# Window attention with a pooled branch: one copy of x, one trip of statistics, key sums on GpSimd, seeds in PSUM

## What is computed

```python
def _gn(v, G=32, eps=1e-05):
    g = v.reshape(B_, G, C_ // G, H_, W_)
    m = jnp.mean(g, axis=(2, 3, 4), keepdims=True)
    s = jnp.var(g, axis=(2, 3, 4), keepdims=True)
    return ((g - m) / jnp.sqrt(s + eps)).reshape(v.shape)

xr = x.reshape(B, H, W, C)                      # a reshape, no transpose
g = window_attn(xr, Wqkv, bqkv, scale) @ Wproj + bproj
l = xr.reshape(B, C, H // 2, 2, W // 2, 2).mean(axis=(3, 5))
l = window_attn(l.reshape(B, h, w, C), Wqkv, bqkv, scale).reshape(B, C, h, w)
lx = 0.5 * (px[:, :, :-1, :] + px[:, :, 1:, :])    # px: l, padded by reflection
ly = 0.5 * (py[..., :-1] + py[..., 1:])
l = jax.image.resize(lx + ly, (B, C, H, W), method='bilinear')
return (g + l.reshape(B, H, W, C)).transpose(0, 3, 1, 2)

x = x + _L0_conv_ref(_gn(x), Wqkv, bqkv, Wproj, bproj)
```

## Time and profile before

| What | Value |
|---|---|
| median of 3 runs | 93.77 us (93.16 to 94.08) |
| span of the profiled execution, first to last instruction | 92.3 us |
| the profiled execution's own time | not given apart; median minus span is 1.5 us |
| busy: PE, VectorE, ScalarE, GpSimd | 79.7, 61.6, 36.6, 26.9 us |
| HBM read, written | 5.11 MB, 2.10 MB |

### The profile page before, as it was taken

One profiled execution on the slowest core, in us unless ns is written; L12 is line 12 of the kernel. 1 busy time (PEld: TensorE's weight loads), 2 busy tenths in 40 slices (PEclk: granted clock), 3 DMA queues, 4 the chain that ended last, 5 costly groups with the idle time before them and its releaser, 6 DMA issues.

```text
span 92.3 us, 1700 instructions
## 1 busy us (share of the span) xinstructions
PE 79.7 (86%) x620; PEld 62.0 (67%) x620; DVE 61.6 (67%) x101; ACT 36.6 (40%) x80; POOL 26.9 (29%) x50
## 2 busy tenths in 40 slices
...
PEclk9999999999999999999999999999999999999999
...
GB/s 6 248 254 251 228 322 404 415 87 0 7 0 0 0 4 0 11 0 0 0 0 0 7 0 0 0 0 0 7 0 227 0 0 4 7 0 227 0 227 227
DMA packets 3464, 7.32 MB, mean 79 GB/s; under 512 B 896, under 2 KB 1152, under 8 KB 3456
## 3 DMA queue, kind: packets, MB, share of 16 engines
...
HBM read 5.11 MB, written 2.10 MB: 78 GB/s over the span
## 4 chain that ended last, share of the span: by engine, by line
PE 74%; DMA 9%; ACT 3%; POOL 3%; DVE 2%; issue 2%; ACTq 2%; DVEq 1%
PE ot_ps L755 14%; PE q_ps L681 9%; PE v_ps L691 9%; DMA xr<-in_x 9%; PE k_ps L672 6%; PE job_ps L771 6%; PE s_ps L713 6%; PE ot_ps L739 5%; PE job_ps L778 5%; PE job_ps L644 4%; PE k_ps L771 2%; ACT xn L431 2%; PE job_ps L656 2%; PE k_ps L778 2%; ACT xt L447 1%
## 5 line engine op out<-in xcount | busy, mean ns | idle before, releaser
L542 DVE TENSOR_TENSOR qk<-q_sb,k_ps 128x1536 f32<-128x1536 f32 x10 | 17.3, 1737 | 2.7 <-ACT q_sb L460 2.7
L410 POOL TENSOR_TENSOR out_sb<-out_sb,xc 128x512 f32<-128x512 f32 x4 | 6.0, 1512 | 40.9 <-ACT out_sb L482 40.9
L590 DVE TENSOR_TENSOR pv<-prob_w,v_ps 128x1536 f32<-128x1536 f32 x9 | 15.7, 1739 | 0.7 <-PE ot_ps L755 0.7
L755 PEld LDWEIGHTS ot_ps<-ident,pv 128*128 128x128 f32 x120 | 13.7, 141 | 3.3 <-issue 3.0
L755 PE MATMUL ot_ps<-ident,pv 128*128 128x128 f32 x120 | 14.9, 273 | 0.0
L477 ACT ACTIVATE ot<-ot_ps,bias_qkv 128x512 f32<-128x512 f32 x10 | 6.9, 687 | 12.8 <-PE ot_ps L755 12.8
L497 DVE BATCH_NORM_STATS2 bn<-xr 128x6 f32<-128x512 f32 x8 | 5.5, 682 | 6.6 <-DMA xr<-in_x 6.6
L681 PE MATMUL q_ps<-xt,w_sb 128*128 128x512 f32 x16 | 9.3, 665 | 0.5 <-ACT xt L447 0.5
L691 PEld LDWEIGHTS v_ps<-w_sb,xt 128*128 128x128 f32 x64 | 7.9, 192 | 1.0 <-issue 1.0
L691 PE MATMUL v_ps<-w_sb,xt 128*128 128x128 f32 x64 | 8.5, 275 | 0.0
L278 POOL TENSOR_TENSOR xn<-xn 128x384 f32<-128x384 f32 x6 | 6.0, 1000 | 8.0 <-ACT xn L431 8.0
...
## 6 DMA issues: line engine op xcount, KB each, us to landing
...
```

The lines of the kernel that those rows point to most:

```text
L542: nc.vector.tensor_tensor(qk[:, m % 2, :, :, n % 2, :], q, k, ALU.mult).then_inc(qk_done, 1)
L590: nc.vector.tensor_tensor(to, p, v, ALU.mult).then_inc(pv_done, 1)
L755: ins = nc.tensor.matmul(view[:, q // 2, q % 2], pv[:, n % 2, q, k, :], eye, is_transpose=True, start=(sums == KEYS and q == 0), stop=last ...
```

## The change

- x is loaded once, by channels (`xc`), one load per image on SP's queue, and serves statistics, pooling, normalising and the last addition. `wp_sb` moves from ScalarE's queue to SP's. `resize_sb` has 8 blocks for 10.
- Statistics: two `bn_stats` and one `bn_aggr` per image, the mean of squares made on VectorE (`ag`), one small matmul per image (`st`), four small VectorE operations (`ps`), the power on GpSimd (`pw`), offset and scale on VectorE (`of`).
- Transposes (`T`) read the channel copy; token 0 is subtracted after the transpose (`df`): on VectorE out of PSUM for tiles 0 to 3, on GpSimd in SBUF for the other six, where ScalarE's `xe` copies all 512 columns (128 for tiles 0 to 3).
- Value 0 of an image tile is projected with the operands exchanged, so that its features lie on the partitions; ScalarE adds the bias (`ve`) and writes it twice for each half of a bank (`sd`), and `O` accumulates on it. `v0` is gone.
- GpSimd adds the three products of the keys in SBUF (`H`, two operations of 128 x 512 for tiles 0, 2, 3, 4, 6, 7 and 8, three with value 0 for the pooled tiles 1 and 5, none for tile 9), so that `O` has 4 transposes for 12, but for tile 9. Pooled tiles get another 2 (`Om`, to the copy `mid`).
- ScalarE writes x and the output bias into the result's bank ahead (`sx`); `L` (4 blocks for 5) and `W` accumulate on it, and a copy (`R`) goes out, on ScalarE but for (3, 0) on VectorE. `add` is gone; image 3 is stored whole.
- The sum of exponents is made by two additions instead of a reduction. Four banks (`a_ps`) are shared by T, Q, K, V, O by a table, three (`b_ps`) by seeds and results; `pv` has four buffers. The pooled tiles stand second and sixth, and `ORDER` is new.

```diff
-TILES = [(0, 0), (0, 1), (1, 0), (None, 0), (1, 1), (2, 0), (None, 1), (2, 1), (3, 0), (3, 1)]
...
+TILES = [(0, 0), (None, 0), (0, 1), (1, 0), (1, 1), (None, 1), (2, 0), (2, 1), (3, 0), (3, 1)]
...
+PV = [1, 3, 0, 2, 3, 1, 0, 2, 0, 3]
...
+ORDER = {
+    "PE": [
+        ("st", 0), ("st", 1), ("T", 0), ("T", 2), ("st", 2), ("Q", 0), ("T", 1), ("K", 0), ("Q", 2), ("Q", 1),
+        ("T", 3), ("st", 3), ("K", 1), ("zero",), ("T", 4), ("K", 2), ("Q", 3), ("S", 0), ("K", 3), ("T", 6),
+        ("T", 9), ("V", 0), ("T", 7), ("S", 1), ("T", 5), ("V", 1), ("Q", 6), ("Q", 4), ("Q", 7), ("T", 8), ("K", 7),
+        ("Q", 9), ("K", 6), ("Q", 5), ("K", 5), ("K", 4), ("S", 3), ("V", 3), ("O", 1), ("O", 0), ("V", 2), ("Om", 1),
+        ("S", 2), ("K", 9), ("V", 4), ("Q", 8), ("L", 1, 0), ("O", 3), ("V", 5), ("W", 1, 0), ("V", 7), ("O", 2),
+        ("V", 6), ("L", 0, 0), ("L", 0, 1), ("K", 8), ("W", 0, 1), ("W", 0, 0), ("O", 4), ("S", 4), ("L", 1, 1),
+        ("V", 9), ("Om", 5), ("O", 5), ("W", 1, 1), ("O", 7), ("L", 2, 1), ("V", 8), ("W", 2, 1), ("O", 6), ("O", 9),
+        ("L", 2, 0), ("W", 2, 0), ("L", 3, 1), ("L", 3, 0), ("O", 8), ("W", 3, 1), ("W", 3, 0),
+    ],
+    "DVE": [
+        ("bn", 0), ("ag", 0), ("bn", 1), ("ps", 0), ("ag", 1), ("bn", 2), ("of", 0), ("nm", 0, 0), ("ps", 1),
+        ("ag", 2), ("df", 0), ("of", 1), ("df", 2), ("ps", 2), ("bn", 3), ("df", 1), ("ag", 3), ("M", 0), ("of", 2),
+        ("ps", 3), ("df", 3), ("M", 1), ("of", 3), ("M", 2), ("X", 0), ("M", 3), ("D", 0), ("U", 0), ("X", 1),
+        ("P", 0), ("P", 1), ("D", 1), ("M", 7), ("M", 6), ("M", 5), ("M", 4), ("U", 1), ("X", 3), ("P", 3), ("P", 2),
+        ("X", 2), ("M", 9), ("D", 2), ("D", 3), ("U", 2), ("P", 4), ("P", 5), ("M", 8), ("U", 3), ("P", 7), ("X", 4),
+        ("P", 6), ("D", 4), ("U", 4), ("P", 9), ("P", 8), ("R", 3, 0),
+    ],
+    "ACT": [
+        ("nm", 0, 1), ("xe", 0), ("pn", 0), ("xe", 2), ("pn", 1), ("Qo", 0), ("xe", 1), ("nm", 1), ("Qo", 2),
+        ("Qo", 1), ("xe", 3), ("xe", 4), ("nm", 2), ("Qo", 3), ("nm", 3), ("pn", 3), ("xe", 6), ("E", 0), ("xe", 9),
+        ("pn", 2), ("xe", 7), ("ve", 0), ("sd", 0), ("xe", 5), ("ve", 1), ("E", 1), ("Qo", 6), ("Qo", 4), ("Qo", 7),
+        ("xe", 8), ("Qo", 9), ("sx", 1, 0), ("Qo", 5), ("oo", 1), ("ve", 3), ("sd", 3), ("oo", 0), ("om", 1),
+        ("ve", 2), ("ve", 4), ("sx", 0, 0), ("E", 2), ("Qo", 8), ("oo", 3), ("E", 3), ("sd", 2), ("oo", 2), ("ve", 5),
+        ("sx", 0, 1), ("R", 1, 0), ("sd", 4), ("ve", 7), ("R", 0, 1), ("R", 0, 0), ("ve", 6), ("sx", 1, 1), ("oo", 4),
+        ("sx", 2, 1), ("E", 4), ("sd", 7), ("om", 5), ("oo", 5), ("ve", 9), ("oo", 7), ("sd", 6), ("R", 1, 1),
+        ("ve", 8), ("sd", 9), ("R", 2, 1), ("sx", 2, 0), ("oo", 6), ("oo", 9), ("sx", 3, 1), ("sx", 3, 0),
+        ("R", 2, 0), ("sd", 8), ("oo", 8), ("R", 3, 1),
+    ],
+    "POOL": [
+        ("p1", 0), ("p2", 0), ("p1", 1), ("pw", 0), ("p1", 3), ("pw", 1), ("p2", 1), ("p2", 3), ("pw", 2), ("pw", 3),
+        ("p1", 2), ("p2", 2), ("keyb",), ("df", 6), ("df", 9), ("df", 7), ("df", 4), ("df", 5), ("H", 0, 0),
+        ("H", 1, 0), ("H", 1, 1), ("H", 1, 2), ("H", 0, 1), ("df", 8), ("H", 3, 0), ("H", 3, 1), ("H", 2, 0),
+        ("H", 2, 1), ("H", 4, 0), ("H", 4, 1), ("H", 5, 0), ("H", 5, 1), ("H", 5, 2), ("H", 7, 0), ("H", 7, 1),
+        ("H", 6, 0), ("H", 6, 1), ("H", 8, 0), ("H", 8, 1),
+    ],
+}
...
+WARM = {("st", 0): 4, ("T", 0): 6}
...
-            sp.dma_start(xr[:, 0, 0, :], x_rows[0, 0]).then_inc(x0_first, 16)
...
+            sp.dma_start(xc[:, 0, :], x_chan[0]).then_inc(x_loaded[0], 16)
+            for b in range(1, B):
+                sp.dma_start(xc[:, b, :], x_chan[b]).then_inc(x_loaded[b], 16)
...
+            def sum_keys(n, i):
+                if i == 0:
+                    pool.wait_ge(pv_done, nth("DVE", ("P", n)))
                 else:
+                    pool.wait_ge(keys_summed, nth("POOL", ("H", n, i - 1)))
+                first = pv[:, PV[n], :, 0, :]
+                if i < 2:
+                    to, other = first, pv[:, PV[n], :, i + 1, :]
                 else:
+                    pool.wait_ge(v0_out, nth("ACT", ("ve", n)))
+                    to = low_sum[:, TILES[n][1], :].rearrange("w (q f) -> w q f", q=WIN)
+                    other = v0[:, n, :].unsqueeze(1).broadcast_to([P, WIN, C])
+                nc.gpsimd.tensor_tensor(to, first, other, ALU.add).then_inc(keys_summed, 1)
...
+            def value_0_seed(n):
+                act.wait_ge(v0_out, nth("ACT", ("ve", n)))
+                b_free(act, ("sd", n))
+                to = b_bank(("sd", n))[:, :].rearrange("f (s m r c) -> f s m r c", s=2, r=2, c=GROUP)
+                at = v0[:, n, :].rearrange("f (m c) -> f m c", c=GROUP)
+                for s in range(2):
+                    ins = nc.scalar.copy(to[:, s], at.unsqueeze(2).broadcast_to([P, 32, 2, GROUP]))
+                ins.then_inc(seeded, 1)
...
+            def input_seed(b, k):
+                act.wait_ge(x_loaded[b], 16)
+                act.wait_ge(bp_loaded, 16)
+                b_free(act, ("sx", b, k))
+                nc.scalar.activation(b_bank(("sx", b, k))[:, :].rearrange("f (s h c) -> f s h c", s=2, h=2),
+                                     result_part(xc, b, k), ACT.Identity, bias=bias_p[:, 0:1]).then_inc(x_seeded, 1)
...
+            def channel_stats(b):
+                dve.wait_ge(bn_done, 2 * nth("DVE", ("bn", b)))
+                nc.vector.bn_aggr(mv[:, b, :], bn[:, b, :, :].rearrange("p h s -> p (h s)")).then_inc(mv_done, 1)
+                dve.wait_ge(mv_done, nth("DVE", ("ag", b)))
+                nc.vector.scalar_tensor_tensor(out=mv[:, b, 1:2], in0=mv[:, b, 0:1], scalar=mv[:, b, 0:1],
+                                               in1=mv[:, b, 1:2], op0=ALU.mult, op1=ALU.add).then_inc(square_done, 1)
...
-                nc.vector.tensor_reduce(denom[:, m % 2, :], by_window(expd[:, m % 2, :]), AX.X,
+                nc.vector.tensor_tensor(pair_sum[:, m % 2, :], e[:, 0:128], e[:, 128:256], ALU.add).then_inc(pair_done, 1)
+                dve.wait_ge(pair_done, done)
+                nc.vector.tensor_tensor(denom[:, m % 2, :], pair_sum[:, m % 2, 0:64], pair_sum[:, m % 2, 64:128],
                                         ALU.add).then_inc(denom_done, 1)
...
+                before = [j[1] for j in among("DVE", "P")]
+                before = [j for j in before[:before.index(n)] if PV[j] == PV[n]]
+                if before and is_low(before[-1]):
+                    dve.wait_ge(keys_summed, nth("POOL", ("H", before[-1], 2)))
+                elif before:
+                    dve.wait_ge(ot_made, nth("PE", ("O", before[-1])))
...
-            def turn_value_0(n):
...
+                left = [0] + list(range(1 + min(len(sums), 2), KEYS))
+                if is_low(n):
+                    a_free(pe, ("O", n))
+                    view = a_bank(("O", n))[:, :].rearrange("f (i l a r c) -> f r l i a c", i=2, l=KL, a=8, r=2)
                     eye = ident[:, :].rearrange("p (i a c) -> p i a c", i=2, a=8)
                 else:
+                    pe.wait_ge(seeded, nth("ACT", ("sd", n)))
+                    view = b_bank(("sd", n))[:, :].rearrange("f (s m r c) -> f r s m c", s=2, m=32, r=2)
+                    eye = ident[:, :].rearrange("p (m c) -> p m c", c=GROUP)
                 for q in range(WIN):
+                    for k in left:
+                        part = low_sum[:, TILES[n][1], q * C:(q + 1) * C] if is_low(n) else pv[:, PV[n], q, k, :]
+                        ins = nc.tensor.matmul(view[:, q // 2, q % 2], part, eye, is_transpose=True,
+                                               start=(is_low(n) and q == 0), stop=(k == left[-1]), skip_group_check=True)
+                ins.then_inc(ot_made, 1)
...
+                for h in range(2):
+                    for s in range(2):
+                        j = 4 * h + 2 * k + s
+                        if FIRST[j] == 64:
+                            values_at = mid[:, b // 2, b % 2 * P:(b % 2 + 1) * P]
+                        else:
+                            at = b % 2 * 256 + FIRST[j]
+                            values_at = ot[:, low, at:at + P]
+                        at = s * 256 + h * P
+                        nc.tensor.matmul(b_bank(("sx", b, k))[:, at:at + P], resize_sb[:, j, :], values_at, start=False,
+                                         stop=True, skip_group_check=True)
```

More of the change, by code:

```diff
@@ L63, in resize_blocks @@
     r = np.kron(up_y @ blur(PH, True), up_x) + np.kron(up_y, up_x @ blur(PW, False))
[L64 to L81, removed]
[8 rows of a table removed]
[L90 to L96, removed]
[4 rows of a table removed]
-    ],
-    "DVE": [
[6 rows of a table removed]
[L109 to L122, removed]
+    r = r.T.reshape(PH * PW, K, P)
+    first = [0, 0, 0, 64, 64, 128, 128, 128]
+    out = np.zeros((P, K, P))
+    for k in range(K):
+        out[:, k] = r[first[k]:first[k] + P, k]
```

(36 more changed lines are left out.)

747 lines of the change are left out of this document (328 added, 419 removed), and 27 rows, old and new, of tables (A_BANK, B_BANK, ORDER).

## The result

The change takes the median from 93.7 us to 89.73 us (89.1 to 90.52, four runs): a ratio of 0.9555, with a 95% interval of 0.9497 to 0.9613. It is faster by 4.5%, where 84.0 us, 10% less, had been forecast: the sign was right, the time lies at the upper end of the range (90.0), and less than half of the gain came. Executions of one kernel differ by 1 to 4 us, and the intervals of the ratio leave out the slower ones. The profiled execution took 89.42 us and has a span of 87.6 us.

The account below looks back on a forecast made before the run. VectorE was to bound: first M 16.6 + VectorE work 50.5 + lock 5 + handoffs 1 = last P 73.1; + 4.9 = last W 78.0; + 4.35 + 0.2 = span 82.5; + 1.5 = 84.0 us, range 79.5 to 90.0.

Parts of the forecast that it names:

- TensorE's sum: TensorE's work after the change: 14.8 us less, 56.2 us remaining, starting at 11 us and not the bound.
- The runs of 4 elements: Transposes' output patterns, runs of 4 elements for 8: costed at nothing; up to 16 us more TensorE work if they slowed it.
- PE busy near 60: Sign expected in the profile after: TensorE's busy figure near 60, with gaps.
- The first `M`: End of the head: first M starts at 16.6 us for 20.1, with image 1 loaded at about 6.4.
- VectorE's sum: VectorE's work from the first M on, added up by mean durations, without stalls: 50.5 us.
- The lock: D's two additions and product wait for GpSimd's sums over SBUF access: 0 to 19.5 us, taken as 5.
- The first rival: The lock in D takes up to 19.5 us; slower from 15 us on, 6%; milder form, 8 to 13 us, 8%.
- I allow 1 us beyond what its slack hides: Main stage: handoffs over ScalarE, between TensorE's and VectorE's steps, add 1 us.
- rival 2: Every M waits 0.9 us for its queries from ScalarE, 9 us: 92, or 86 to 92 for half; 11%.
- ScalarE: about 56 passes of 512 elements at 0.69: ScalarE's work, smaller passes included, comes to 47 us for 36.6, second to VectorE.
- After the last `W`: End of the kernel, last result and store: 4.35 us as before, plus 0.2 for the larger store.
- Rival 3: TensorE stays the bound through doubled output costs (89 us) or idles on shared banks (within 1% of old time, 4%).

Follow-up runs that it names:

- f1_both: Changed kernel with x seeds and results walking SBUF in pairs of neighbours, and the key bias difference made earlier in GpSimd's list: 82.88 us, ratio 0.8791.
- f2_three: As f1_both, with the sum of exponents as one reduction in the place of two additions: 78.25 us, ratio 0.8341.
- f4_both_nosums: As f1_both, without GpSimd's key sums for the seven image tiles, whose O has 12 transposes again: 86.68 us, ratio 0.9204.
- e2_keyb: Changed kernel with the key bias difference ahead of the fourth power and the pooling of image 2 in GpSimd's list: 85.11 us, ratio 0.9102.
- h1_fill: Changed kernel with ten filling matmuls on TensorE ahead of its wait for the key bias, the wait kept: 88.26 us, ratio 0.928.
- e1_pairs: Changed kernel with ScalarE's seeds of x and the results walking SBUF in pairs of neighbours, the jumps made in PSUM: 87.05 us.

## Why the forecast was wrong in size

The direction and most prices held; of the new bound a part. VectorE sets the pace of the main stage, since 4.4 us less of its work took 3.3 out of it (f1_both to f2_three), but TensorE is almost level: 6.1 us more of its work cost 3.8 (`f4_both_nosums`), and the chain up to 70 us runs through its pieces. The profiled 89.42 us stand 5.4 above 84.0, and the steps account for them:

- **TensorE's sum**: the prices of the pieces were right; a K is still 0.65 and four transposes 0.44. The runs of 4 elements cost nothing, also as said: twelve transposes take 1.50 us in the timeline (73.43) and took 1.47 in the old one's. The sign "PE busy near 60" did not come, 70.1 was measured: 6.7 us of it lie before 11 us, some 2 are the half clock, and the filling ahead of `T` 0 was not counted. From 11 us to the last `W` PE is busy for 61.7 us in e2_keyb, where the clock holds, and was for 74.8 in the old kernel: 13 us less for the forecast 14.8. It costs nothing in the sum below.
- **The first `M`** at 17.31 for 16.6: +0.7. Image 1 was there at 8.05 and not at 6.4. A term of the head was too small; VectorE waited 2.0 us for it.
- **VectorE's sum** of 50.5 by mean durations was too large: neighbouring rows overlap (two `P` in 3.41 us, not 3.49), -1.9 over the stage. This term was not measured by itself; it is the difference that the other terms leave.
- **The lock**, 5 us: right. Additions and product ran 0.544, 0.746 and 0.558 us where their undisturbed rows are 0.28, 0.22 and 0.36: 5 x 0.99 = 4.9. How it goes, in the changed kernel:

```profile
37.57 0.28 DVE L573 TENSOR_TENSOR pair_sum<-expd 128x128 f32<-128x128 f32 x1
37.73 2.61 POOL L402 TENSOR_TENSOR pv<-pv 128x512 f32<-128x512 f32 x2 [0.39 <-DVE pv L612]
...
37.89 1.19 DVE L575 TENSOR_TENSOR denom<-pair_sum 128x64 f32<-128x64 f32 x1
...
39.12 0.55 DVE L578 RECIPROCAL inv<-denom 128x64 f32<-128x64 f32 x1
...
39.70 0.86 DVE L580 TENSOR_TENSOR prob<-expd,inv 128x192 f32<-128x192 f32 x1
```

The second addition, 0.22 us of work, starts at 37.89 just behind a sum of 1.27 us (the first of two, from 37.73) and ends with it, at 39.08; the product, at 39.70, ends just behind the second. In f4_both_nosums, where GpSimd sums only for the pooled tiles, the same addition is long beside the one such sum that it meets (at 35.88 us) and short without:

```profile
36.04 1.19 DVE L571 TENSOR_TENSOR denom<-pair_sum 128x64 f32<-128x64 f32 x1
...
52.89 0.23 DVE L571 TENSOR_TENSOR denom<-pair_sum 128x64 f32<-128x64 f32 x1
```

So it is the sums that hold it up. The first rival named the place and the mechanism; the price stayed far from the 15 us at which it decides. `f2_three` showed what the edit of `D` was worth: 4.4 us of VectorE's work, 3.3 us of time.
- **"I allow 1 us beyond what its slack hides"** for handoffs: this is the first step that failed. VectorE's gaps were 4.2 us (2.27, 1.67, 0.22), +3.2. They were not of rival 2's kind (no `M` waited for ScalarE's queries). The cause lies in GpSimd's list, where `keyb` now stands behind a power that hangs on the last image's statistics. The prediction walked VectorE's list in the head and not GpSimd's and TensorE's, and never priced `zero`. `e2_keyb` took 4.6 us off the time (4.1 off the stage), of which `h1_fill` gives 1.6 to the clock.
- **"ScalarE: about 56 passes of 512 elements at 0.69"**: the second. Fifteen of them, seeds of x and results, took 1.2 and 1.1, which is 8 x 0.52 + 7 x 0.42 = 7 us more ScalarE work. In the middle it is hidden; at the end it is not: last `P` to last `W` 8.4 us for 4.9, +3.5. The price was read from L477, which is contiguous on both sides, though the old kernel's own result pass, with pairs in SBUF, was there too:

```profile
L482 ACT ACTIVATE out_sb<-job_ps,bias_p 128x512 f32<-128x512 f32 x4 | 2.9, 734 | 3.0 <-PE job_ps L778 3.0
```

Its stride would have raised the question. `e1_pairs` took 2.7 of the 3.5; what is left is ScalarE's order and TensorE's blocks.
- **After the last `W`** 4.1 us for 4.55, -0.4, and 1.8 outside the span for 1.5, +0.3.

Sum: 0.7 - 1.9 + 3.2 + 3.5 - 0.4 + 0.3 = 5.4. It closes because the second term was taken as what is left. That the time still fell within the range of 79.5 to 90.0 is the width of the range: two terms missed by over 3 us each, and neither was the one that the range was widened for.

Rival 3 said that TensorE could stay the bound; `f4_both_nosums` shows how near it is. The best kernel found is f2_three, three small edits on top of the change: 78.3 us, 16.6% under the kernel before (0.8341, 0.828 to 0.8402).
